# Gated layer over a context of 257 keys: chunks of 128 + 128 + 1 in place of three of 86

## The chip, the cores and the metric

The kernel runs on one core of a Trainium2 chip. The metric is device time in microseconds of the whole program, one launch. Everything is fp32.

## The reference, cut to what matters

```python
def _L0_xattn_ref(x, w1, v1, w2):            # x: (128, 32, 128); all three weights are ctx: (128, 257, 128)
    h1 = jnp.einsum('eth,efh->etf', x, w1)
    h2 = jnp.einsum('eth,efh->etf', x, v1)
    g = jax.nn.gelu(h1, approximate=False) * h2
    return jnp.einsum('etf,efh->eth', g, w2)
...
x = x + _L0_xattn_ref(_layernorm(x, axis=-1), ctx_1024, ctx_1024, ctx_1024)
x = x + _L0_attn_ref(...)      # and four more layers, which the change leaves alone
```

For each of 128 batches, 32 rows of x are normalised and multiplied with the 257 keys of the batch's context, which gives h of 32 by 257. Since h1 and h2 are the same, g is gelu(h) * h. Then g is multiplied with the context again, and the result is added to x.

## The kernel before, in words

The function `stage_ctx_glu` computes this layer. A tile `t` is four batches, 4 x 32 = 128 rows of X, and there are NT = 32 tiles; X stays in SBUF as `k.X` for the whole kernel. The context of a tile is loaded as `cN` ("glu_ctx_N", four buffers in turn), as three chunks of 86 keys (JC = 86, NJ = 3; the 258th is zero) in 96 partitions. The host lays it out in `layouts`.

Per tile, the steps are:

- `ctx_transpose`: TensorE transposes the chunks of each batch (12 a tile, L248) into banks `pC[b]`; ScalarE copies batches 0 and 2 (L308), VectorE 1 and 3 (L359) to `cT`.
- `norm` (VectorE, L353), `transpose` (TensorE, L241) and `copy` (ScalarE, L303) prepare the normalised, transposed rows `xT`.
- `h`: four matmuls (L257) of one batch each, on four groups of 32 columns of the array at once. Each matmul is recorded as two instructions.
- `gelu` (ScalarE, L313) and `gate` (VectorE, L364) make gh.
- `g_transpose`: three transposes (L265), `g_copy` by ScalarE (L318).
- `y`: for each chunk, four matmuls (L274), one a batch, which again run side by side: 12 matmuls, 24 instructions.
- `add`: VectorE adds `y` to X (L109) and takes the statistics of the new X for the next layer (L111).

Each engine runs its own instruction list, and semaphores order them. Within a list the order is written out by hand in `body`. TensorE's is: context transposes of tile t+1, transposes of gh of t, `h` of t+1, `transpose` of t+2, `y` of t. VectorE's is: copies of t+1, `norm` of t+2, `gate` of t+1, `add` of t. The first four tiles and the last four are written out; those between run in a loop of four tiles a round (`tiles`).

X is loaded in four groups of 4, 8, 10 and 10 tiles (GROUPS), all ahead of or between the first four context loads on the one queue of SyncE (SP). `look_at(g)` is VectorE's statistics of a group (L344, L347), and POOL then computes the reciprocal deviation of the group (L403, L405, waited for by `norm` of tiles 0 and 4). `look_at(1)` stands in tile 0 ahead of its `gate`, `look_at(2)` and `look_at(3)` at the start of tiles 1 and 2. A context buffer is loaded again when `y` of its tile is done (L212).

Of the kernel before, what the change touches and what calls it, by code (L numbers as in the profile page):

```python
# [24 lines left out]
P = 128  # L25
# [127 lines left out]

def stage_ctx_glu(nc, k, x, ident, ctxN, ahead):
    JZ = NJ * JC
    with ExitStack() as ctx:
# [5 lines left out]
        def sem(name):  # L162
# [8 lines left out]
        ge = [sb(f"gelu{i}", [P, JZ]) for i in range(2)]  # L171
        gh = [sb(f"gh{i}", [P, JZ]) for i in range(2)]
        gT = [sb(f"gh_T{i}", [JC, NJ * P]) for i in range(2)]
# [4 lines left out]
        x_landed, ident_landed = [sem(f"x_landed{g}") for g in range(len(GROUPS))], sem("ident_landed")  # L178
        stats, means, var_eps, rstd_done, set_up = (sem(n) for n in (
            "stats0", "mean_var_done", "variance_shifted", "rstd_done", "constants_set"))  # L180
# [18 lines left out]
        @block.sync  # L199
        def _(sp):  # L200
            clear_stale(sp, k)

            def load(t, slot):
                sp.dma_start(cN[slot][:, :, :, :], ctxN[t]).then_inc(landed[slot], 16)
# [12 lines left out]

        def tiles(eng, body):

            for t in range(WAYS):  # L220
                body(t, t)
            with eng.Fori(0, NT // WAYS - 2) as i:
                for w in range(WAYS):
                    body(WAYS * i + WAYS + w, w)
            for w in range(WAYS):
                body(NT - WAYS + w, w)
# [10 lines left out]
        def _(pe):  # L237
# [5 lines left out]
            def ctx_transpose(t, slot, b):  # L243
                if b == 0:
                    pe.wait_ge(landed[slot], turn(t, slot))
                wait(pe, (c_even, c_odd)[b % 2], 2 * (t - 1) + b // 2 + 1)
                for c in range(NJ):
                    m = pe.transpose(pC[b][:, c * JC:(c + 1) * JC], cN[slot][0:JC, b, c, :], k.ident[0:JC, 0:JC])  # L248
                m.then_inc(c_turned, 1)

            def h(t, slot):
                pe.wait_ge(xt_ready, t + 1)
                pe.wait_ge(c_even, 2 * t + 2)
                pe.wait_ge(c_odd, 2 * t + 2)
                wait(pe, gh_ready, t)
                for b in range(BT):
                    m = pe.matmul(pH[b * S:(b + 1) * S, 0:JZ], xT[slot % 2][:, b * S:(b + 1) * S],  # L257
                                  cT[slot % 2][:, b, :], start=True, stop=True)
                m.then_inc(h_ready, 1)

            def g_transpose(t, slot):
                pe.wait_ge(gh_ready, t + 1)
                wait(pe, gt_ready, t)
                for c in range(NJ):
                    m = pe.transpose(pG[0:JC, c * P:(c + 1) * P], gh[slot % 2][:, c * JC:(c + 1) * JC], k.ident[:, :])  # L265
                m.then_inc(g_turned, 1)

            def y(t, slot):
                pe.wait_ge(gt_ready, t + 1)
                wait(pe, added, 2 * (t - 1) + 1)  # L270
                for c in range(NJ):
                    for b in range(BT):
                        o = c * P + b * S
                        m = pe.matmul(pY[b * S:(b + 1) * S, 0:D], gT[slot % 2][:, o:o + S],  # L274
                                      cN[slot][0:JC, b, c, :], start=(c == 0), stop=(c == NJ - 1))
                m.then_inc(y_ready, 1)

            def body(t, slot):
                nxt, second = after(t, slot, 1), after(t, slot, 2)
                if isinstance(t, int) and t == 0:  # L280
                    pe.wait_ge(ident_landed, 16)
                    for b in range(BT):
# [12 lines left out]
                y(t, slot)  # L295
# [3 lines left out]
        def _(act):  # L299
# [5 lines left out]
            def ctx_copy(t, slot, b):  # L305
                act.wait_ge(c_turned, BT * t + b + 1)
                wait(act, h_ready, t - 1)
                act.activation(cT[slot % 2][:, b, :], pC[b][:, 0:JZ], ACT.Copy).then_inc(c_even, 1)  # L308

            def gelu(t, slot):  # L310
                act.wait_ge(h_ready, t + 1)
                wait(act, gh_ready, t - 1)
                act.activation(ge[slot % 2][:, :], pH[:, 0:JZ], ACT.Gelu).then_inc(ge_ready, 1)  # L313

            def g_copy(t, slot):
                act.wait_ge(g_turned, t + 1)
                wait(act, y_ready, t - 1)
                act.activation(gT[slot % 2][:, :], pG[0:JC, 0:NJ * P], ACT.Copy).then_inc(gt_ready, 1)  # L318

            def body(t, slot):  # L320
                nxt, second = after(t, slot, 1), after(t, slot, 2)
                if isinstance(t, int) and t == 0:
                    ctx_copy(t, slot, 0)
                    ctx_copy(t, slot, 2)
# [14 lines left out]
        def _(dve):  # L339
# [9 lines left out]
            def norm(t, slot):  # L349
                if isinstance(t, int) and t in (0, 4):  # L350
                    dve.wait_ge(rstd_done, 1 if t == 0 else len(GROUPS))
                wait(dve, turned, t - 1)
# [3 lines left out]
            def ctx_copy(t, slot, b):  # L356
                dve.wait_ge(c_turned, BT * t + b + 1)
                wait(dve, h_ready, t - 1)
                dve.tensor_copy(cT[slot % 2][:, b, :], pC[b][:, 0:JZ]).then_inc(c_odd, 1)  # L359

            def gate(t, slot):
                dve.wait_ge(ge_ready, t + 1)
                wait(dve, g_turned, t - 1)
                dve.tensor_tensor(gh[slot % 2][:, :], ge[slot % 2][:, :], pH[:, 0:JZ], ALU.mult).then_inc(gh_ready, 1)  # L364
# [33 lines left out]
        def _(pool):  # L398
            pool.memset(half_neg[:, :], -0.5).then_inc(set_up, 1)
            pool.wait_ge(set_up, 1)  # L400
            for g, (lo, hi) in enumerate(GROUPS):
# [3 lines left out]
                pool.tensor_tensor(k.RSTD[:, lo:hi], k.SD[:, lo:hi], half_neg[:, lo:hi], ALU.pow).then_inc(rstd_done, 1)  # L405


# [2094 lines left out]
def build(nc, a, out):  # L2502
    with ExitStack() as ctx:
# [21 lines left out]
        with ExitStack() as early:  # L2525
            def eb(name, shape):
# [22 lines left out]
                gqa, ("gqa_wq", "gqa_wkv", "gqa_wout", "gqa_gamma", "gqa_normw", "causal"))]  # L2549
            stage_ctx_glu(nc, k, a["x"], a["ident"], a["ctxN"], for_linear)  # L2550
            deviation_phase(nc, k, "ln2")
# [34 lines left out]
def layouts(i):  # L2586
# [7 lines left out]
    o["ctxT"] = ctx.reshape(NT, BT, JP, D).transpose(0, 3, 1, 2)  # L2594
    ctx_rows = np.zeros((NT, JR, BT, NJ, D), np.float32)
    ctx_rows[:, :JC] = ctx.reshape(NT, BT, NJ, JC, D).transpose(0, 3, 1, 2, 4)
    o["ctxN"] = ctx_rows
    row = np.arange(P)
# [74 lines left out]
```

## Time and profile before

| | |
|---|---|
| median of 3 runs | 2311.27 us (2311.0 to 2311.86) |
| the profiled execution | 2309.65 us, of which its span 2307.9 |
| mean granted TensorE clock over the span | 0.966 |
| busy share of the span | TensorE 92%, VectorE 67%, ScalarE 56%, POOL 45% |
| last VectorE instruction of this stage | starts at 135.40 us |
| first TensorE instruction of the next stage | starts at 138.17 us |

The span is the time from the first instruction of the program to the last. Busy shares are means over all stages. A line such as L257 is a line of the kernel; the same helper line can serve several stages (L109 and L111 do). A matmul's end is modelled, so the starts of TensorE's groups tell more than their ends.

### The profile page before, as it was taken

The page shows a single profiled execution, that of the slowest core. Times are in us where ns is not written, and L with a number is a line of the kernel's source. Part 1 is how long each engine was busy: PE and PEld are TensorE (multiplying, and loading weights), DVE is VectorE, ACT ScalarE, POOL GpSimd, SP SyncE. Part 2 cuts the span into 40 slices and gives each one's busy share as a digit, 9 for nine tenths or more (in the row PEclk, how much of TensorE's full clock was granted, in tenths as well). Part 3 has the DMA queues.
Part 4 walks back from the last instruction along what each step waited for, and adds up shares of the span by engine and source line. Part 5 has one row for each costly group of instructions (what it writes and reads, how often), then busy time and mean ns, then how long its engine had stood idle before and what let it go on. Part 6 is the DMA issues. An engine that isn't in the chain of part 4 may idle for free. (4 is left out here: it accounts for less than half of the span.)

```text
span 2307.9 us, 81023 instructions
## 1 busy us (share of the span) xinstructions
PE 2119.3 (92%) x27948; PEld 1563.2 (68%) x27949; DVE 1535.6 (67%) x5463; ACT 1300.8 (56%) x3747; POOL 1027.1 (45%) x935
## 2 busy tenths in 40 slices
PE   7989999997999899978999999999889999989994
PEld 4657777774677677756777777777556665665992
DVE  4578888874777743347888888888666666754442
ACT  3555555555888433336777777777645555532330
POOL 1024444333888300006555656555266666625115
PEclk9999999997999899988999999999999999979997
DMA  6640000000000000000111111111140000001112
GB/s 161 174 130 1 0 0 0 0 1 1 1 0 0 1 1 0 0 26 25 36 34 34 34 34 34 34 34 34 35 169 0 0 0 0 0 2 41 42 42 77
DMA packets 41208, 71.52 MB, mean 31 GB/s; under 512 B 6176, under 2 KB 30624, under 8 KB 40480
## 3 DMA queue, kind: packets, MB, share of 16 engines
q1 hardware_dynamic: 37792, 63.55, 9.4%
q0 software_dynamic: 3328, 6.82, 0.9%
q8 instruction: 53, 0.87, 0.2%
q14 instruction: 35, 0.29, 0.0%
HBM read 60.91 MB, written 9.44 MB: 30 GB/s over the span
## 5 line engine op out<-in xcount | busy, mean ns | idle before, releaser
L2276 ACT ACTIVATE xat_scores<-xat_scores,xat_least 128x257 f32<-128x257 f32 x512 | 258.5, 505 | 103.5 <-DVE xat_least L2410 102.3
L2410 DVE CUSTOM_DVE_ANT_0 xat_scores<-bank,xat_mask_b 128x257 f32<-128x257 f32 x512 | 207.6, 422 | 88.7 <-PE bank L2120 87.9
L1050 POOL TENSOR_TENSOR gqa_rnorm<-gqa_norm_min,gqa_minus_half 128x12 f32<-128x12 f32 x64 | 145.8, 2278 | 104.9 <-DVE gqa_norm_min L1127 104.9
L2178 PE MATMUL bank<-ident,xat_scores 128*128 128x128 f32 x1024 | 189.2, 287 | 0.0
L2178 PEld LDWEIGHTS bank<-ident,xat_scores 128*128 128x128 f32 x1024 | 116.4, 142 | 81.0 <-issue 49.0
L690 POOL TENSOR_TENSOR lin_q_softmax<-lin_q_exp,lin_q_rsum 128x512 f32<-128x512 f32 x64 | 66.7, 1042 | 223.2 <-DVE lin_q_rsum L751 223.2
L1693 DVE SCALAR_TENSOR_TENSOR X<-bank,expert_shares,X 128x128 f32 (+1 forms) x256 | 72.0, 343 | 130.9 <-PE bank L1607 130.7
L1630 ACT ACTIVATE moe_gelu<-bank 128x512 f32<-128x512 f32 x128 | 76.5, 597 | 146.1 <-PE bank L1597 146.1
L1607 PEld LDWEIGHTS bank<-moe_w,moe_gelu 128*128 128x128 f32 x1024 | 124.2, 192 | 30.8 <-issue 18.2
L1368 POOL TENSOR_TENSOR bat_scores<-bat_scores,bat_max 128x512 f32<-128x512 f32 x128 | 130.5, 1041 | 32.5 <-DVE bat_max L1400 32.5
L1400 DVE CUSTOM_DVE_ANT_0 bat_scores<-bank,bat_causal_add 128x128 f32<-128x128 f32 x512 | 110.7, 286 | 47.2 <-PE bank L1256 47.2
L568 PEld LDWEIGHTS bank<-lin_w_v_out,lin_z_T 128*128 128x128 f32 x1024 | 119.1, 191 | 22.0 <-issue 20.2
L568 PE MATMUL bank<-lin_w_v_out,lin_z_T 128*128 128x128 f32 x1024 | 131.2, 281 | 1.3 <-ACT lin_z_T L620 1.3
L1607 PE MATMUL bank<-moe_w,moe_gelu 128*128 128x128 f32 x1024 | 124.6, 275 | 0.3 <-DVE expert_shares L1680 0.3
L1597 PE MATMUL bank<-ln_T,moe_w 128*128 (+1 forms) x256 | 123.0, 604 | 0.8 <-PEq L1423 0.8
L2295 ACT ACTIVATE xat_p_T<-bank 128x256 f32<-128x256 f32 x256 | 96.4, 377 | 41.3 <-PE bank L2178 38.0
L2342 POOL TENSOR_TENSOR xat_ctx_kept<-xat_keep,xat_ctx_T 128x1028 f32<-128x1028 f32 x32 | 71.0, 2220 | 82.9 <-DMA xat_ctx_T<-in_ctxT 82.8
L2120 PE MATMUL bank<-xat_k_cos,xat_q_blocks 32*128 32x257 f32 x1024 | 92.7, 431 | 16.6 <-DVE xat_least L2410 14.7
L2366 POOL TENSOR_SCALAR xat_keep<-xat_pad 128x1028 f32<-128x1028 uint8 x1 | 1.6, 1552 | 237.6 <-DMA xat_pad<-in_xat_pad 237.6
L2417 DVE COPY xat_p_T<-bank 128x256 f32<-128x256 f32 x256 | 106.7, 417 | 0.2 <-PE bank L2178 0.2
L2276 ACT ACTIVATION_READ_ACCUMULATOR xat_scores<-xat_scores,xat_least 128x1 f32 x512 | 97.6, 191 | 0.0
L2151 PE MATMUL bank<-xat_w_v,xat_ctx_T 128*128 128x128 f32 x512 | 90.2, 299 | 0.0
(320 smaller groups left out, 5826.9 us busy)
## 6 DMA issues: line engine op xcount, KB each, us to landing
glu_ctx_N<-in_ctxN SPq DMA_DIRECT2D x32, 576.0 KB, 4.3
xat_ctx_T<-in_ctxT SPq DMA_DIRECT2D x32, 516.0 KB, 3.6
xat_pad<-in_xat_pad SPq DMA_DIRECT2D x32, 128.5 KB, 3.4
expert_w<-in_glx_w SPq DMA_DIRECT2D x1, 4096.0 KB, 14.9
slot_rows<-gqa_zero_rows SPq DMA_DIRECT2D x1, 2560.0 KB, 11.0
slt_rows<-slot_rows SPq DMA_DIRECT2D x40, 64.0 KB, 1.8
slot_results<-slt_y POOLq DMA_DIRECT2D x40, 64.0 KB, 1.8
moe_w<-in_moe_w SPq DMA_DIRECT2D x2, 1024.0 KB, 5.8
```

The lines of the kernel that those rows point to most:

```text
L568: m = pe.matmul(pY[:, 0:D], zT[slot][:, hd, :], wvo[:, hd // 2, hd % 2, :], start=(hd == 0), stop=(hd == H - 1))
L1050: pool.tensor_tensor(rn[h][:, :], sm[h][:, :], half_neg[:, :], ALU.pow).then_inc(rnorm, 1)
L1368: pool.tensor_tensor(sx[g][:, :, :], sx[g][:, :, :], spread(mx[g][:, :], P), ALU.subtract).then_inc(s_shifted, 1)
L1400: dve.tensor_tensor_reduce(sx[g][:, i, :], pS[g][:, i * P:(i + 1) * P], cadd[:, :], 1.0, -BIG, ALU.add, ALU.max, mx[g][:, i:i + 1]).then_i ...
L1597: pe.matmul(pH[e % 2][c][:, :], w1[:, e, c * P:(c + 1) * P], k.LT[:, ts(b, TB), :], start=True, stop=True).then_inc(h_made, 1)
L1607: m = pe.matmul(pY[e % WAYS][:, i * D:(i + 1) * D], ge[e % 2][:, c, i * P:(i + 1) * P], w2[:, e, c, :], start=(c == 0), stop=(c == NF - 1))
L2120: m = pe.matmul(pS[g][:, 0:J], qb[slot][r, part, j, :, :], keys[j % 2][r, :], start=(part == 0), stop=(part == 1))
L2178: m = pe.transpose(dst[:, c * P:(c + 1) * P], sx[j % 2][:, g, c * P:(c + 1) * P], k.ident[:, :])
L2276: act.activation(sx[j % 2][:, g, :], sx[j % 2][:, g, :], ACT.Exp, bias=mn[j % 2][g][:, 0:1], scale=-1.0, accum_out=sm[j % 2][:, g:g + 1]). ...
L2295: act.activation(pt[j % 2][g][:, :], unit_bank(*at)[:, 0:NC * P], ACT.Copy).then_inc(pa_copied, 1)
L2410: dve.tensor_tensor_reduce(sx[j % 2][:, g, :], pS[g][:, 0:J], mb[slot][:, j, :], 1.0, BIG, ALU.add, ALU.min, mn[j % 2][g][:, 0:1]).then_in ...
L2417: dve.tensor_copy(pt[j % 2][g][:, :], unit_bank(*at)[:, 0:NC * P]).then_inc(pd_copied, 1)
```

## The change

The 257 keys are split as 128 + 128 + 1. The two full chunks take the same way as before, with 8 transposes of the context, 2 of gh and 8 matmuls in `y` a tile. The last key goes another way. Its rows for all 128 batches are loaded once (`lN`, 64 KB), transposed once (`lT`), and POOL puts the four columns of a tile into `cT` (`put_last`), so `h` still has all keys. For `y`, the host lays the last key's row 32 times a batch beside the two chunks (the load stays 576 KB), and VectorE multiplies it with the last column of gh and adds it to X (`add_last`), before `add`. The X groups 2 and 3 are loaded behind all of the first four context tiles, their `look_at` moves to tiles 3 and 4, behind `gate` and `add_last` and ahead of `add`, and `look_at(1)` behind `gate` and `add_last` of tile 0. POOL's deviations follow, and eight tiles are written out at the start instead of four.

```diff
-        cN = [sb(f"ctx_N{i}", [JR, BT, NJ, D]) for i in range(WAYS)]
-        cT = [sb(f"ctx_T{i}", [P, BT, JZ]) for i in range(2)]
+        cN = [sb(f"ctx_N{i}", [P, BT * NC + 1, D]) for i in range(WAYS)]
+        cT = [sb(f"ctx_T{i}", [P, BT, J]) for i in range(2)]
+        lN, lT = sb("last_N", [P, D]), sb("last_T", [P, P])
...
+            sp.dma_start(lN[:, :], ctx_last).then_inc(lasts_landed, 16)
...
-            for t, (lo, hi) in enumerate(GROUPS):
-                sp.dma_start(k.X[:, lo:hi, :], x_rows[:, lo:hi, :]).then_inc(x_landed[t], 16)
-                load(t, t)
+            load_x(0)
+            load(0, 0)
+            load_x(1)
+            load(1, 1)
+            load(2, 2)
+            load(3, 3)
+            load_x(2)
+            load_x(3)
             with sp.Fori(0, NT // WAYS - 1) as i:
                 for w in range(WAYS):
                     sp.wait_ge(y_ready, WAYS * i + w + 1)
+                    sp.wait_ge(last_added, WAYS * i + w + 1)
                     load(WAYS * i + w + WAYS, w)
...
-                for c in range(NJ):
-                    m = pe.transpose(pC[b][:, c * JC:(c + 1) * JC], cN[slot][0:JC, b, c, :], k.ident[0:JC, 0:JC])
+                for c in range(NC):
+                    m = pe.transpose(pC[b][:, c * P:(c + 1) * P], cN[slot][:, b * NC + c, :], k.ident[:, :])
...
+                pe.wait_ge(last_put, t + 1)
                 wait(pe, gh_ready, t)
...
-                for c in range(NJ):
+                for c in range(NC):
                     for b in range(BT):
                         o = c * P + b * S
                         m = pe.matmul(pY[b * S:(b + 1) * S, 0:D], gT[slot % 2][:, o:o + S],
-                                      cN[slot][0:JC, b, c, :], start=(c == 0), stop=(c == NJ - 1))
+                                      cN[slot][:, b * NC + c, :], start=(c == 0), stop=(c == NC - 1))
...
+            def add_last(t, slot):
+                dve.wait_ge(gh_ready, t + 1)
+                dve.scalar_tensor_tensor(out=k.X[:, t, :], in0=cN[slot][:, BT * NC, :], scalar=gh[slot % 2][:, LAST:J],
+                                         in1=k.X[:, t, :], op0=ALU.mult, op1=ALU.add).then_inc(last_added, 1)
 
             def add(t, slot):
                 dve.wait_ge(y_ready, t + 1)
+                dve.wait_ge(last_added, t + 1)
                 residual_tile(dve, k, t, pY[:, 0:D], added, 2 * t)
...
+                    gate(t, slot)
+                    add_last(t, slot)
                     look_at(1)
-                    gate(t, slot)
-                if isinstance(t, int) and 1 <= t < 3:
-                    look_at(t + 1)
...
                 if nxt:
                     gate(*nxt)
+                    add_last(*nxt)
+                if isinstance(t, int) and t in (3, 4):
+                    look_at(t - 1)
...
+            def put_last(t, slot):
+                wait(pool, h_ready, t - 1)
+                pool.tensor_copy(cT[slot % 2][:, :, LAST], lT[:, ts(t, BT)]).then_inc(last_put, 1)
...
+                if isinstance(t, int) and t in (0, 4, 5):
+                    deviation({0: 1, 4: 2, 5: 3}[t])
```

## Rows read from the trace of the kernel before

**Rows 1.** Timeline of one settled tile: start us, us, engine, line, operation
```profile
86.47 0.64 PE L257 MATMUL bank<-glu_ctx_T,glu_xT 128*32 128x258 f32 x8 [0.29 <-issue]
...
87.17 0.39 ACT L313 ACTIVATE glu_gelu<-bank 128x258 f32<-128x258 f32 x1 [0.47 <-PE bank L257]
87.30 0.86 PE L274 MATMUL bank<-glu_ctx_N,glu_gh_T 86*32 86x128 f32 x24
...
87.59 0.42 DVE L364 TENSOR_TENSOR glu_gh<-glu_gelu,bank 128x258 f32<-128x258 f32 x1 [0.97 <-ACT glu_gelu L313]
88.09 1.11 PE L248 MATMUL bank<-ident,glu_ctx_N 86*128 86x86 f32 x12
88.34 0.29 DVE L109 TENSOR_TENSOR X<-X,bank 128x128 f32 x1 [0.33 <-PE bank L274]
...
88.77 0.29 DVE L111 BATCH_NORM_STATS2 bn_stats<-X  x1
...
88.98 0.74 DVE L359 COPY glu_ctx_T<-bank 128x258 f32<-128x258 f32 x2
...
89.82 0.64 PE L257 MATMUL bank<-glu_ctx_T,glu_xT 128*32 128x258 f32 x8 [0.29 <-issue]
```

**Rows 2.** Timeline of ScalarE: the gelu of tile 7 and of tile 31
```profile
49.80 0.39 ACT L313 ACTIVATE glu_gelu<-bank 128x258 f32<-128x258 f32 x1 [0.46 <-PE bank L257]
...
131.32 0.39 ACT L313 ACTIVATE glu_gelu<-bank 128x258 f32<-128x258 f32 x1 [0.57 <-PE bank L257]
```

**Rows 3.** Timeline of an early tile, number 4
```profile
33.13 1.98 PE L248 MATMUL bank<-ident,glu_ctx_N 86*128 86x86 f32 x12
...
35.84 1.09 PE L257 MATMUL bank<-glu_ctx_T,glu_xT 128*32 128x258 f32 x8
...
37.26 1.51 PE L274 MATMUL bank<-glu_ctx_N,glu_gh_T 86*32 86x128 f32 x24
...
37.40 0.42 DVE L364 TENSOR_TENSOR glu_gh<-glu_gelu,bank 128x258 f32<-128x258 f32 x1 [1.56 <-ACT glu_gelu L313]
38.70 1.55 PE L248 MATMUL bank<-ident,glu_ctx_N 86*128 86x86 f32 x9
```

**Rows 4.** Timelines of VectorE and TensorE in the first six tiles
```profile
12.81 0.42 DVE L364 TENSOR_TENSOR glu_gh<-glu_gelu,bank 128x258 f32<-128x258 f32 x1 [0.47 <-ACT glu_gelu L313]
...
14.92 1.09 PE L257 MATMUL bank<-glu_ctx_T,glu_xT 128*32 128x258 f32 x8
...
18.45 2.01 DVE L344 BATCH_NORM_STATS2 bn_stats<-X 128x6 f32<-128x128 f32 x10
...
21.19 0.72 DVE L359 COPY glu_ctx_T<-bank 128x258 f32<-128x258 f32 x2
...
22.17 1.09 PE L257 MATMUL bank<-glu_ctx_T,glu_xT 128*32 128x258 f32 x8 [1.76 <-DVE glu_ctx_T L359]
...
41.26 1.09 PE L257 MATMUL bank<-glu_ctx_T,glu_xT 128*32 128x258 f32 x8
...
45.75 0.64 PE L257 MATMUL bank<-glu_ctx_T,glu_xT 128*32 128x258 f32 x8 [0.30 <-issue]
```

**Rows 5.** Timeline of TensorE in the next stage: transposes of 128 by 128
```profile
158.06 0.60 PE L531 MATMUL bank<-ident,lin_q_softmax 128*128 128x128 f32 x4
```

**Rows 6.** Groups of VectorE by form, cross attention: busy us, mean ns, idle before
```profile
L2430 DVE SCALAR_TENSOR_TENSOR xat_o_mixed<-xat_v,xat_v_last,bank 128x128 f32<-128x128 f32 x128 | 43.4, 339 | 1.2 <-PE bank L2142 1.2
```

**Rows 7.** Timeline of VectorE in the linear attention's loop
```profile
301.32 0.68 DVE L749 TENSOR_REDUCE lin_q_sum<-lin_q_exp 128x8 f32<-128x512 f32 x1
302.03 0.20 DVE L751 RECIPROCAL lin_q_rsum<-lin_q_sum 128x8 f32<-128x8 f32 x1
```

**Rows 8.** Groups of POOL by form
```profile
L1379 POOL TENSOR_SCALAR bat_head_diag_scaled<-bat_head_diag 128x4 f32<-128x4 f32 x1 | 0.2, 198 | 0.1
```

**Rows 9.** The page's DMA issues: count, KB each, median us to landing
```profile
glu_ctx_N<-in_ctxN SPq DMA_DIRECT2D x32, 576.0 KB, 4.3
```

**Rows 10.** A stretch of transposes: us; PE, PEld, DVE, ACT, POOL busy; clock; DMA
```profile
534.00:542.00 8.00, 8.00 (x23) 3.98 (x22) 4.39 (x18) 8.00 (x23) 0.00 (x0) 0.50 0.00 0
```

More of the change, by code:

```diff
@@ L151, in _, with stage_ctx_glu @@
                 dve.tensor_tensor(dst[:, :], k.RSTD[:, :], k.MS[:, :], ALU.mult).then_inc(rc, 1)
-def stage_ctx_glu(nc, k, x, ident, ctxN, ahead):
-    JZ = NJ * JC
+def stage_ctx_glu(nc, k, x, ident, ctxN, ctx_last, ahead):
+    NC, LAST = 2, J - 1
+    JF = NC * P
     with ExitStack() as ctx:
@@ L166, in stage_ctx_glu @@
         WAYS = 4
-        cN = [sb(f"ctx_N{i}", [JR, BT, NJ, D]) for i in range(WAYS)]
-        cT = [sb(f"ctx_T{i}", [P, BT, JZ]) for i in range(2)]
+        cN = [sb(f"ctx_N{i}", [P, BT * NC + 1, D]) for i in range(WAYS)]
+        cT = [sb(f"ctx_T{i}", [P, BT, J]) for i in range(2)]
+        lN, lT = sb("last_N", [P, D]), sb("last_T", [P, P])
         xn = [sb(f"xn{i}", [P, D]) for i in range(2)]
         xT = [sb(f"xT{i}", [P, P]) for i in range(2)]
-        ge = [sb(f"gelu{i}", [P, JZ]) for i in range(2)]
-        gh = [sb(f"gh{i}", [P, JZ]) for i in range(2)]
-        gT = [sb(f"gh_T{i}", [JC, NJ * P]) for i in range(2)]
+        ge = [sb(f"gelu{i}", [P, J]) for i in range(2)]
+        gh = [sb(f"gh{i}", [P, J]) for i in range(2)]
+        gT = [sb(f"gh_T{i}", [P, NC * P]) for i in range(2)]
         pX, pG, pY, pH = k.bank[0], k.bank[5], k.bank[6], k.bank[7]
@@ L218, in tiles @@
         def tiles(eng, body):
-            for t in range(WAYS):
-                body(t, t)
-            with eng.Fori(0, NT // WAYS - 2) as i:
+            for t in range(2 * WAYS):
+                body(t, t % WAYS)
+            with eng.Fori(0, NT // WAYS - 3) as i:
                 for w in range(WAYS):
-                    body(WAYS * i + WAYS + w, w)
+                    body(WAYS * i + 2 * WAYS + w, w)
             for w in range(WAYS):
@@ L254, in h @@
                 pe.wait_ge(c_odd, 2 * t + 2)
+                pe.wait_ge(last_put, t + 1)
                 wait(pe, gh_ready, t)
                 for b in range(BT):
-                    m = pe.matmul(pH[b * S:(b + 1) * S, 0:JZ], xT[slot % 2][:, b * S:(b + 1) * S],
+                    m = pe.matmul(pH[b * S:(b + 1) * S, 0:J], xT[slot % 2][:, b * S:(b + 1) * S],
                                   cT[slot % 2][:, b, :], start=True, stop=True)
@@ L263, in g_transpose @@
                 wait(pe, gt_ready, t)
-                for c in range(NJ):
-                    m = pe.transpose(pG[0:JC, c * P:(c + 1) * P], gh[slot % 2][:, c * JC:(c + 1) * JC], k.ident[:, :])
+                for c in range(NC):
+                    m = pe.transpose(pG[:, c * P:(c + 1) * P], gh[slot % 2][:, c * P:(c + 1) * P], k.ident[:, :])
                 m.then_inc(g_turned, 1)
@@ L270, in y @@
                 wait(pe, added, 2 * (t - 1) + 1)
-                for c in range(NJ):
+                for c in range(NC):
                     for b in range(BT):
@@ L281, in body @@
                     pe.wait_ge(ident_landed, 16)
+                    pe.wait_ge(lasts_landed, 16)
+                    pe.transpose(pG[:, 0:P], lN[:, :], k.ident[:, :]).then_inc(lasts_turned, 1)
                     for b in range(BT):
@@ L307, in ctx_copy @@
                 wait(act, h_ready, t - 1)
-                act.activation(cT[slot % 2][:, b, :], pC[b][:, 0:JZ], ACT.Copy).then_inc(c_even, 1)
+                act.activation(cT[slot % 2][:, b, 0:JF], pC[b][:, 0:JF], ACT.Copy).then_inc(c_even, 1)
             def gelu(t, slot):
@@ L312, in gelu @@
                 wait(act, gh_ready, t - 1)
-                act.activation(ge[slot % 2][:, :], pH[:, 0:JZ], ACT.Gelu).then_inc(ge_ready, 1)
+                act.activation(ge[slot % 2][:, :], pH[:, 0:J], ACT.Gelu).then_inc(ge_ready, 1)
             def g_copy(t, slot):
@@ L317, in g_copy @@
                 wait(act, y_ready, t - 1)
-                act.activation(gT[slot % 2][:, :], pG[0:JC, 0:NJ * P], ACT.Copy).then_inc(gt_ready, 1)
+                act.activation(gT[slot % 2][:, :], pG[:, 0:NC * P], ACT.Copy).then_inc(gt_ready, 1)
             def body(t, slot):
@@ L349, in norm @@
             def norm(t, slot):
-                if isinstance(t, int) and t in (0, 4):
-                    dve.wait_ge(rstd_done, 1 if t == 0 else len(GROUPS))
+                if isinstance(t, int) and t in (0, 4, 8):
+                    dve.wait_ge(rstd_done, {0: 1, 4: 2, 8: len(GROUPS)}[t])
                 wait(dve, turned, t - 1)
@@ L358, in ctx_copy @@
                 wait(dve, h_ready, t - 1)
-                dve.tensor_copy(cT[slot % 2][:, b, :], pC[b][:, 0:JZ]).then_inc(c_odd, 1)
+                dve.tensor_copy(cT[slot % 2][:, b, 0:JF], pC[b][:, 0:JF]).then_inc(c_odd, 1)
             def gate(t, slot):
@@ L400, in _, with deviation @@
             pool.wait_ge(set_up, 1)
-            for g, (lo, hi) in enumerate(GROUPS):
+            def deviation(g):
+                lo, hi = GROUPS[g]
                 pool.wait_ge(means, hi)
@@ L405, in _, with body @@
                 pool.tensor_tensor(k.RSTD[:, lo:hi], k.SD[:, lo:hi], half_neg[:, lo:hi], ALU.pow).then_inc(rstd_done, 1)
+            def put_last(t, slot):
+                wait(pool, h_ready, t - 1)
+                pool.tensor_copy(cT[slot % 2][:, :, LAST], lT[:, ts(t, BT)]).then_inc(last_put, 1)
+            def body(t, slot):
+                nxt = after(t, slot, 1)
+                if isinstance(t, int) and t == 0:
+                    deviation(0)
+                    pool.wait_ge(lasts_copied, 1)
+                    put_last(t, slot)
+                if nxt:
+                    put_last(*nxt)
+                if isinstance(t, int) and t in (0, 4, 5):
+                    deviation({0: 1, 4: 2, 5: 3}[t])
+            tiles(pool, body)
 def unit(t, h):
@@ L2594, in layouts @@
     o["ctxT"] = ctx.reshape(NT, BT, JP, D).transpose(0, 3, 1, 2)
-    ctx_rows = np.zeros((NT, JR, BT, NJ, D), np.float32)
-    ctx_rows[:, :JC] = ctx.reshape(NT, BT, NJ, JC, D).transpose(0, 3, 1, 2, 4)
-    o["ctxN"] = ctx_rows
+    chunks, lasts = g["ctx_1024"][:, :J - 1].reshape(NT, BT, 2, P, D), g["ctx_1024"][:, J - 1]
+    spread_last = np.repeat(lasts.reshape(NT, BT, D), S, axis=1)
+    o["ctxN"] = np.concatenate([chunks.transpose(0, 3, 1, 2, 4).reshape(NT, P, 2 * BT, D), spread_last[:, :, None]], 2)
+    o["ctx_last"] = lasts
     row = np.arange(P)
```

13 lines of the change are left out of this document (10 added, 3 removed).

## The prediction

> **What bounds the kernel now.** The change touches one stage, the first, which holds 32 tiles of the kernel's 81,023 instructions and ends near 135 of 2307.9 us; everything behind it is the same code. So I read that stage alone: first the order of instructions over time for one settled tile, then the same for the first tiles, then single prices elsewhere.
>
> In a settled tile [rows 1] the first TensorE matmul `h` (L257) starts at 86.47 and that of the next tile at 89.82, a period of 3.35 us. Call the start of `h` zero. ScalarE's gelu (L313) starts at 0.70, VectorE's `gate` (L364) at 1.12 and ends at 1.54. TensorE's second matmul `y` (L274) starts at 0.83 and the transposes of the context tile follow at 1.62 (88.09). VectorE's `add` (L109) waits for `y` and starts at 1.87, so VectorE stands idle from 1.54 to 1.87. From there the way is fixed: add, a gap of 0.14, statistics, two copies (L359) from 2.51 to 3.25, and `h` of the next tile 0.10 later. Add to next `h` is 1.48. TensorE's context transposes (1.11 with their tail) and the transposes of gh fit beside that. The reader is to see a ring: h, y, add, statistics, copies, h. TensorE looks nearly full, but only `h`, the transpose between and `y` lie on the ring.
>
> The gelu rows 24 tiles apart [rows 2] give (131.32 - 49.80)/24 = 3.397 us a tile, the same ring with the loop's branch in one tile of four.
>
> The first tiles run at the lower of TensorE's two levels. The granted clock cannot be read there (it is recorded as 1.00 from the start), but the instructions can: 12 context transposes take 1.98 us against 1.11, `y` runs from 37.26 to 38.70, 1.44 against 0.79, and the tile takes 38.70 - 33.13 = 5.57 [rows 1, 3]. There TensorE is the bound. On top come stalls: `look_at` (statistics over a group of X) sits on VectorE ahead of its copies, 18.45 to 21.19, 2.74 us for ten tiles of X, and holds `h` back by 1.76 [rows 4]. The first one in the loop, of eight tiles of X (L377), stands ahead of tile 0's `gate` (12.81), which waits for a gelu that comes late anyway; it costs nothing. `h` starts at 14.92 for tile 1, 22.17 for tile 2, 35.84 for tile 4, 41.26 for tile 5, 45.75 for tile 6 [rows 3, 4] and 0.70 before its gelu, 49.10, for tile 7 [rows 2]. From tile 6 on its eight instructions take 0.64 instead of 1.09: the upper level.
>
> **The change, part by part, settled tiles.**
> Context transposes go from 12 of 86 rows to 8 of 128. Four transposes of 128 by 128 take 0.60 us with their tail [rows 5], so eight take at most 1.20, and less by one tail; against 1.11 that is between -0.1 and +0.1, and it lies off the ring, where TensorE stands still before `h`.
> The transposes of gh go from 3 to 2 and their copy from 384 to 256 columns: off the ring.
> `y` goes from 24 instructions in three rounds of four batches to 16 in two: 0.79 x 1/3 = 0.26 us less, on the ring. `add` could start at 1.87 - 0.26 = 1.61.
> The new `add_last` (VectorE, 128 x 128, with a scalar from each row) stands between `gate` and `add`, and `add` waits for it. The nearest row is the same trick in the cross attention, 339 ns, 128 times [rows 6]. It reads gh, so it waits for `gate`; an instruction that waits for the one before it with one wait starts 0.03 after its end (L749 ends at 302.00, L751 starts at 302.03) [rows 7], with two waits 0.14 after it (88.34 + 0.29 to 88.77) [rows 1]. So `add` starts at 1.54 + 0.03 + 0.34 + 0.03 = 1.94 at best and at 1.54 + 0.14 + 0.34 + 0.14 = 2.16 at worst. That is later than 1.61, and later than today's 1.87: **the ring moves from y to gate, add_last, add.** The period grows by 0.07 to 0.29. `gate` has one wait that matters and in `add` the wait for `add_last` is the last of two, which speaks for the lower end; that the two waits ahead of the statistics do cost 0.14 in every tile of the loop speaks for a bit more. I take 0.13. From tile 7 to tile 31 that is 24 x 0.13 = **+3.1 us** (1.7 to 7.0). The last tile's add stands behind an add_last too, +0.3.
>
> The Trainium skill (VectorE: DVE Perf Modes, section The TRN2 errata) gives an fp32 operation on two tensors (N + 151)/0.96 ns, 291 ns at 128 elements; the trace agrees for L109, 0.29. By that rule add_last would take 0.29 instead of 0.34, and 24 tiles would give 1.2 us less.
>
> POOL's `put_last`, a copy of 4 elements a partition, is bounded by 198 ns from a row of the same size [rows 8] and one tile ahead of its use. In tiles 4 and 5 a `deviation` stands before the next put_last on POOL (about 2.2 us), still 4 us ahead of the `h` that waits for it. If that cover were gone it would cost those 2.2 once. Loads keep their 576 KB and land in 4.3 us [rows 9], while a slot is free three tiles, 10 us, before it is read; the new wait of SP's queue for add_last comes before y is ready, and what is queued behind it is only the next load. The two late X loads have until tile 3. Hidden: nothing.
>
> **The first tiles.** The extra 64 KB (rows of the last key) stands before the first tile's load: about 0.25 us. `gate` of tile 0 ends at 12.81 + 0.42 + 0.27 = 13.5, add_last at 13.9; then the first `look_at`, now behind them, 8/10 of 2.74 = 2.2, then copies and gap 0.85: `h` of tile 1 at 17.0 instead of 14.92, **+2.1**. Tiles at the lower level need 5.57 less 0.48 for `y` less 0.25 for one transpose of gh (1.98/12 for 86 columns, so 0.25 for 128), 4.8. A tile with a `look_at` needs 1.98 to the end of gate (37.40 + 0.42 - 35.84) + 0.37 + 2.74 + 0.32 + 0.21 + 0.84 = 6.5. So tile 5 starts at 17.0 + 3 x 4.8 + 6.5 = 37.9 (before 41.26, **-3.3**), tile 6 at 44.4 (before 45.75), because its look_at now falls where there was none. If TensorE were at its upper level from there, tile 7 would start at 47.9, **-1.2**. But both look_at tiles leave it idle for over 2 us just before, and each tile at the lower level costs 4.8 - 3.5 = 1.3. I count one such tile: +0.1 for the whole start.
>
> Sum: +0.1 + 3.1 + 0.3 = **+3.5 us**. The profiled execution took 2309.65 (2307.9 of span, 1.75 around it), so 2313.2 for the like of it; the median of the three runs is 1.6 higher, 2311.27, hence **2314.8**.
>
> **Rivals.**
> *The long chain on VectorE and a later clock (slower).* Both gaps at 0.14 give 24 x 0.29 = 7.0, +7.4 in all: 2318.7. For it: the loop's waits on register values often show 0.14. Chance 0.2.
> *TensorE stays at its lower level (slower).* The change takes away a third of `y` and leaves the streamed columns of the transposes as they are. A stretch of nothing but transposes ran at clock 0.50 although TensorE was busy for all of its 8.00 us [rows 10]. Each further tile costs 1.3: one more gives +4.8, the bound of 0.2%; all 24, 2314.8 + 30 = 2345. Against it: h and y still come every tile, and once risen the level held through the 24 tiles of [rows 2]. The Trainium skill (TensorE: Matmul & The Clock Gate, Part 4, PE-mode transpose) says that transposes do not count as TensorE work for the clock in the same way; by this rule the rise comes later or not at all, and the trace agrees with its premise by that 0.50. Chance 0.18 for at least one more tile than I count.
> *The opposite: the stalls end sooner and the clock rises early.* With the look_ats moved to tiles 3 and 4, TensorE works without a stall from 17.0 to 34. If it rises there and holds, two or three tiles gain 1.3 each and the start is worth -3 to -5: 2309.5 to 2311.5, no change. Against it are the idle times right behind. Chance 0.12.
> *y's saving shows (faster).* If gate, add_last and their waits took 0.07 instead of 0.40, `add` would follow `y` at 1.61: 24 x -0.26 = -6.2, with -1.2 from the start -7.4: 2303.9. It decides from `add` earlier than 1.82 on. Only an add_last that overlaps its own input would do it. Chance 0.07.
> The forecast itself holds 0.43.
>
> **How the numbers follow.** What a measurement can tell from no change is 0.2%, 4.6 us. Faster: the last rival and a sliver of the early clock, 0.09. Slower by over 4.6: the first two and the upper part of my own range (2311 to 2317), 0.41. Within: 0.50. The range reaches from the early clock, 2309, to the long chain with two or three late tiles, 2322; outside stay y's saving below and a clock that hardly rises above, together under 0.2.
>
> **What would show it.** VectorE: L109's successor starting right behind add_last and no longer waiting for TensorE; period 3.45 to 3.6 where it was 3.40. `y` at 0.53. TensorE's idle time a tile up from 0.3 to 0.7 or more. `h` of tile 1 at 17.0, of tile 5 near 38, of tile 6 near 44. The transposes' 12 to 8 without effect on `h`. Wrong would be: add waiting for `y` as before; a period under 3.35; the level of the clock changing elsewhere than between tiles 5 and 8; POOL or a DMA named before `h`.

## The result and the profile after

The changed kernel takes 2305.59 us (median of 15 runs, 2301.32 to 2310.82), the kernel before 2310.78 on the same chip (15 runs, 2303.7 to 2314.19). The ratio is 0.9982, 95% interval 0.9974 to 0.9991: 0.18% faster, inside the 0.2% that I called no change, but under the lower end of my range, 2309. The profiled execution took 2305.04 us, its span 2303.3.

Timeline of one settled tile after (start us, us, engine, line, operation), the answer to [rows 1]:

```profile
86.55 0.64 PE L273 MATMUL bank<-glu_ctx_T,glu_xT 128*32 128x257 f32 x8 [0.60 <-ACT glu_ctx_T L326]
...
87.25 0.39 ACT L331 ACTIVATE glu_gelu<-bank 128x257 f32<-128x257 f32 x1 [0.87 <-PE bank L273]
87.38 0.38 PEld L290 LDWEIGHTS bank<-glu_ctx_N,glu_gh_T 128*32 128x32 f32 x16
87.38 0.64 PE L290 MATMUL bank<-glu_ctx_N,glu_gh_T 128*32 128x128 f32 x16
87.39 0.19 POOL L439 COPY glu_ctx_T<-glu_last_T 128x4 f32 x1 [3.13 <-PE bank L273]
...
87.67 0.42 DVE L384 TENSOR_TENSOR glu_gh<-glu_gelu,bank 128x257 f32<-128x257 f32 x1 [0.96 <-ACT glu_gelu L331]
...
87.96 1.09 PE L263 MATMUL bank<-ident,glu_ctx_N 128*128 128x128 f32 x8
88.13 0.35 DVE L388 SCALAR_TENSOR_TENSOR X<-glu_ctx_N,glu_gh,X 128x128 f32 x1
...
88.40 0.28 DVE L109 TENSOR_TENSOR X<-X,bank 128x128 f32 x1
...
88.82 0.29 DVE L111 BATCH_NORM_STATS2 bn_stats<-X  x1
...
89.03 0.73 DVE L379 COPY glu_ctx_T<-bank 128x256 f32<-128x256 f32 x2
```

The gate (L384) starts 1.12 after `h`, as before. The `add_last` (L388) follows 0.46 later and takes 0.35, where its row in the cross attention said 0.34 [rows 6]. (The estimate of 0.29 by the formula in the Trainium skill, VectorE: DVE Perf Modes, section The TRN2 errata, is near L109's 0.28, but not near this 0.35.) But `add` (L109) starts 0.27 after the *start* of add_last, 0.08 before its recorded end, at 88.40, which is 1.85 after `h`. Before it stood at 1.87. No releaser stands behind L109 now: it no longer waits for TensorE, only for its turn. The statistics (L111) need the new X and start 0.42 after the start of `add`.

That one VectorE instruction can start before the recorded end of the one ahead could be seen in the kernel before. Timeline of VectorE in its last tiles, which are written out and not in the loop:

```profile
131.74 0.42 DVE L364 TENSOR_TENSOR glu_gh<-glu_gelu,bank 128x258 f32<-128x258 f32 x1 [1.38 <-ACT glu_gelu L313]
132.08 0.28 DVE L109 TENSOR_TENSOR X<-X,bank 128x128 f32<-128x128 f32 x1
132.39 0.29 DVE L111 BATCH_NORM_STATS2 bn_stats<-X 128x6 f32<-128x128 f32 x1
```

The add, which doesn't need this gate's result, starts 0.34 after the start of an instruction of 0.42. And the statistics start 0.03 after the end of add, where the same instructions in the loop show 0.14 [rows 1]. So the number of waits, by which I chose between 0.03 and 0.14, is not what sets that gap.

Timelines of the changed kernel: ScalarE's gelu of tiles 7 and 31, and TensorE's `h` of tiles 1 to 7 (the one number more, [n <-issue], is idle time ahead of it):

```profile
46.22 0.39 ACT L331 ACTIVATE glu_gelu<-bank 128x257 f32<-128x257 f32 x1 [0.73 <-PE bank L273]
...
128.24 0.39 ACT L331 ACTIVATE glu_gelu<-bank 128x257 f32<-128x257 f32 x1 [0.87 <-PE bank L273]
```

```profile
16.08 1.08 PE L273 MATMUL bank<-glu_ctx_T,glu_xT 128*32 128x257 f32 x8 [2.60 <-issue]
...
21.16 0.97 PE L273 MATMUL bank<-glu_ctx_T,glu_xT 128*32 128x257 f32 x8 [0.25 <-issue]
...
24.81 0.64 PE L273 MATMUL bank<-glu_ctx_T,glu_xT 128*32 128x257 f32 x8 [0.60 <-ACT glu_ctx_T L326]
...
28.12 0.64 PE L273 MATMUL bank<-glu_ctx_T,glu_xT 128*32 128x257 f32 x8 [0.60 <-ACT glu_ctx_T L326]
...
34.20 0.64 PE L273 MATMUL bank<-glu_ctx_T,glu_xT 128*32 128x257 f32 x8 [3.35 <-issue]
...
40.24 1.08 PE L273 MATMUL bank<-glu_ctx_T,glu_xT 128*32 128x257 f32 x8 [2.24 <-issue]
...
45.31 0.84 PE L273 MATMUL bank<-glu_ctx_T,glu_xT 128*32 128x257 f32 x8 [0.25 <-issue]
```

The settled period is (128.24 - 46.22)/24 = 3.418 us, against 3.397 [rows 2]: 24 tiles cost +0.5, where I forecast +3.1. This +0.5 doesn't come from `add`: by the gelu rows the two middle tiles of a loop round take 3.32 and 3.31 (before 3.35 and 3.30), but the tile in which the loop turns takes 3.73 and the one behind it 3.42 (before 3.56 and 3.35). In the kernel before with nothing but idle instructions added (the padded kernel below) the turn takes 3.67, so at least a part of this is not the work of the stage. The written-out tiles at both ends give some of it back. Tile 7 starts at 45.31 against 49.10: the start gives -3.8, where I forecast +0.1. In the `h` rows 1.08 is the lower level of the clock (1.2 GHz) and 0.64 the upper (2.4 GHz). TensorE reached the upper one at 21.9 us, worked in it (`h` of tile 2 to 3 took 3.65 us, 3 to 4 took 3.31), fell back at 35.5 during the two look_at tiles (34.20 - 28.12 = 6.08, then 6.04) and rose again at 45.8. The granted clock of two windows of the changed kernel says the same (columns: stretch; its length; busy PE, PEld, DVE, ACT, POOL; clock; DMA share and GB/s):

```profile
30.00:45.00 15.00, 9.40 (x78) 6.29 (x76) 11.10 (x59) 4.30 (x12) 4.80 (x7) 0.68 0.33 102
45.00:60.00 15.00, 12.21 (x158) 7.71 (x161) 9.25 (x30) 7.55 (x23) 0.96 (x5) 0.97 0.54 168
```

The stage's last VectorE instruction starts at 132.71 (135.40 before), -2.7. Nothing behind it was changed, and there the executions scatter by themselves. The mark for the end of the stage is the start of ScalarE's L129 (`std`): 137.15 before, 134.46 after. From it to the end of the span it is 2170.8 us before, 2168.8 after, and 2167.4 to 2173.4 in four profiles below (those without the long last stage told of there, the padded kernel left out). So each experiment is read at the end of the stage first. One part of it is not scatter. From this mark to the next `std` (L133, 528.8 before) the changed kernel, the chunks alone and the kernel with the extra matmuls need 393.1 to 393.6 us in four profiles, all others 391.0 to 392.0; the changed kernel's clock is at 0.50 from 156 to 158 us, the one before at 1.00. What brings that fall is not shown.

### The profile page after: what moved, and what is told of

Read it like the earlier page. It is cut to its first block and busy times, and to the rows that moved or that the text cites. A ratio compares the mean times of both kernels' runs of the same rounds, so it can differ in the third digit from the quotient of the medians.

```text
span 2303.3 us, 80324 instructions
## 1 busy us (share of the span) xinstructions
PE 2102.4 (91%) x27533; PEld 1549.2 (67%) x27534; DVE 1543.0 (67%) x5495; ACT 1297.1 (56%) x3748; POOL 1032.8 (45%) x967
## 5 line engine op out<-in xcount | busy, mean ns | idle before, releaser
L2166 PE MATMUL bank<-xat_k_cos,xat_q_blocks 32*128 32x257 f32 x1024 | 92.7, 431 | 16.6 <-DVE xat_least L2456 14.7
```

The costliest lines, as they stand in the source:

```text
L2166: m = pe.matmul(pS[g][:, 0:J], qb[slot][r, part, j, :, :], keys[j % 2][r, :], start=(part == 0), stop=(part == 1))
```

## The experiments

Twelve runs follow. They were taken in four sittings, and in two of them every profile shows a last stage of 295 to 301 us where it is 258 to 260 otherwise; the median of the kernel before was 2349.5 to 2349.9 there. (Runs under one chip number show both; why it is so stays open.) Ratios are to the kernel before in the same sitting.

**Once more the changed kernel.**

> The kernel after, unchanged, to have it beside the others on one chip. Stage one ends (first instruction of the deviation behind it) at 134.5 us as before, give or take one early tile at the other clock level (2.2 us); ratio to before 0.998.

2343.69, ratio 0.9972 (0.9963 to 0.9981), stage end 133.62. Clock: up at 20.9, down at 34.5, up at 44.8, as in the first profile. Only here there was one more short rise ahead of it: `h` of tile 1 already took 0.64, at 16.26, and the level was lost at 17.5. So the pattern repeats in the main, with 0.8 us between two stage ends of the same kernel.

**add_last ahead of the next gate.**

```diff
                 if second:
                     norm(*second)
+                add_last(t, slot)
                 if nxt:
                     gate(*nxt)
-                    add_last(*nxt)
```

> The kernel after with one move: add_last of tile t stands ahead of gate of tile t+1, in VectorE's idle time, instead of gate and add_last of t+1 ahead of add of t. Theory A (add of tile t does not wait for the add_last in front of it, whose tile is the next one; it only stands behind it in VectorE's queue, at 0.27 us, and y is done before): add then follows y at about 1.6 us after h instead of 1.85, the settled period falls from 3.43 to about 3.1 us, 24 tiles give -8 us against the kernel after, near 2298. Theory B (h is held by ScalarE's copies, as the wait's name says, and VectorE's queue does not matter): period stays at 3.4, no difference.

2339.89, ratio 0.9963 (0.9948 to 0.9977), stage end 126.28. Timeline of a settled tile, and the gelu of tiles 7 and 31:

```profile
78.68 0.64 PE L273 MATMUL bank<-glu_ctx_T,glu_xT 128*32 128x257 f32 x8 [0.35 <-ACT glu_ctx_T L326]
78.75 0.35 DVE L388 SCALAR_TENSOR_TENSOR X<-glu_ctx_N,glu_gh,X 128x128 f32 x1
...
79.51 0.64 PE L290 MATMUL bank<-glu_ctx_N,glu_gh_T 128*32 128x128 f32 x16
...
79.80 0.42 DVE L384 TENSOR_TENSOR glu_gh<-glu_gelu,bank 128x257 f32<-128x257 f32 x1 [0.70 <-ACT glu_gelu L331]
...
80.22 0.29 DVE L109 TENSOR_TENSOR X<-X,bank 128x128 f32 x1
```

```profile
44.77 0.39 ACT L331 ACTIVATE glu_gelu<-bank 128x257 f32<-128x257 f32 x1 [0.73 <-PE bank L273]
...
120.32 0.39 ACT L331 ACTIVATE glu_gelu<-bank 128x257 f32<-128x257 f32 x1 [0.77 <-PE bank L273]
```

The period falls to 3.148. `add` stands 1.54 after `h`, right behind the gate, and add_last runs in VectorE's idle time while `h` is under way. So what the changed kernel pays is the place of add_last in the queue, 0.27 us a tile, and that eats up what the change had gained there, 3.397 - 3.148 = 0.25.

**Without add_last** (the last key's share of `y` is left out, and with it the two waits for add_last).

```diff
                 if nxt:
                     gate(*nxt)
-                    add_last(*nxt)
```

> The kernel after without add_last: the last key's share of y is left out, h and gelu still have it. Theory A: the same as with add_last moved, period about 3.1, -8 us against the kernel after; the difference of the two is what the moved add_last still costs, at most 0.05 us a tile. Theory B: period stays at 3.4.

2419.71, ratio 1.0302 (1.0274 to 1.0331): 70 us slower than the kernel before, although the stage ended at 125.62 with a period of 3.175. All the loss lay in the cross attention, 712 us instead of 636, whose code I had not touched. (The cross attention is taken from the first transpose of its rows to the `std` behind it, 1031.3 to 1667.1 in the kernel before.) That was unexplained then.

**The order alone**: the loads, the look_ats and the eight written-out tiles of the change, with the old chunks of 86.

```diff
-            for t, (lo, hi) in enumerate(GROUPS):
-                sp.dma_start(k.X[:, lo:hi, :], x_rows[:, lo:hi, :]).then_inc(x_landed[t], 16)
-                load(t, t)
+            load_x(0)
+            load(0, 0)
+            load_x(1)
+            load(1, 1)
+            load(2, 2)
+            load(3, 3)
+            load_x(2)
+            load_x(3)
```

> The kernel before (three chunks of 86) with only the order of the change: late X loads behind the four context loads, look_at of groups 2 and 3 in tiles 3 and 4 behind gate, look_at of group 1 behind the first gate, eight tiles written out. Theory C (the order alone brings the early gain, because TensorE works without a stall in tiles 1 to 4 and rises to its upper level): settled period 3.40 as before, tile 7 starts 2 us or more earlier than 49.1. Theory D (it is the work taken off TensorE and the faster loads in 128 partitions): with tiles of 5.57 and two of 7.2, and 17.0 for tile 1, tile 7 starts near 51 and the kernel is 1 to 3 us slower than before.

2433.87, ratio 1.0361 (1.0344 to 1.0379). The same loss in the cross attention (715 us), and the first stage ended 5.0 us *later* than before, at 142.13.

**The chunks alone**: the new chunks, last key included, with the old order of loads and look_ats.

> The kernel after with the loads, look_at and deviations in the order of the kernel before: the chunks alone. Theory C: the stalls of tiles 1 and 2 come back (h of tiles 2 and 3 about 7 us apart each), tile 7 starts at 48 to 50, settled period 3.43, so the kernel is level with before or up to 1 us slower. Theory D: tile 7 starts near 46, and the kernel is as fast as the kernel after. Context loads in 128 partitions land faster than in 96 in both.

2343.9, ratio 0.9977 (0.9968 to 0.9987). Timelines of ScalarE, and of TensorE's `h` of tiles 1 to 4:

```profile
42.61 0.39 ACT L331 ACTIVATE glu_gelu<-bank 128x257 f32<-128x257 f32 x1 [0.89 <-PE bank L273]
...
124.64 0.39 ACT L331 ACTIVATE glu_gelu<-bank 128x257 f32<-128x257 f32 x1 [0.88 <-PE bank L273]
...
130.87 0.32 ACT L129 ACTIVATE std<-mean_var,eps 128x32 f32<-128x32 f32 x1
```

```profile
13.54 0.96 PE L273 MATMUL bank<-glu_ctx_T,glu_xT 128*32 128x257 f32 x8 [0.39 <-issue]
...
19.90 0.64 PE L273 MATMUL bank<-glu_ctx_T,glu_xT 128*32 128x257 f32 x8 [3.32 <-issue]
...
25.94 1.09 PE L273 MATMUL bank<-glu_ctx_T,glu_xT 128*32 128x257 f32 x8 [2.07 <-issue]
...
31.92 0.64 PE L273 MATMUL bank<-glu_ctx_T,glu_xT 128*32 128x257 f32 x8 [0.36 <-issue]
```

Its stage ended 6.3 us ahead of the kernel before (5.7 by a second profile of that one), and 2.8 to 3.6 ahead of the full change. So the gain is the chunks'; the new order takes about half of it back. Most of that stands already at `h` of tile 1, 13.54 against 16.08 in the changed kernel: the first look_at, moved behind the gate. The upper level comes early in the old order too: it was there from about 14 to 21 us, was lost at the look_ats, and came back for good at 31. The whole times don't separate this run from the changed kernel; the stage does.

**Eight more matmuls on TensorE while it waits for the first context tile.**

```diff
+                    for _ in range(8):
+                        pe.matmul(pY[:, 0:P], k.ident[:, :], lN[:, :], start=True, stop=True)
```

> The kernel after with eight extra matmuls of 128 columns (each two instructions, 0.2 us each at the lower level, 3.4 us in all) on data that has landed, in the time before the first context tile lands at 7.0. If only TensorE's level makes the first tiles slow and it rises with such work: the first context transposes already take 1.1 us instead of 2.0 and stage one ends 2 to 4 us earlier than 134.5. If the stalls of VectorE set the first tiles: under 1 us.

2342.26, ratio 0.9969 (0.9959 to 0.998), stage end 134.14. The upper level was there at 7.8 us, and was lost again at 14.6. Timeline of TensorE:

```profile
9.84 0.64 PE L273 MATMUL bank<-glu_ctx_T,glu_xT 128*32 128x257 f32 x8
...
15.71 1.09 PE L273 MATMUL bank<-glu_ctx_T,glu_xT 128*32 128x257 f32 x8 [2.97 <-issue]
```

`h` of tile 0 ran at the upper level, that of tile 1 at the lower one, behind 2.97 us of idle time under `look_at(1)`. Here the early rise was worth nothing: the stage ended between the two ends of the unchanged kernel (133.62 and 134.46), since VectorE stopped TensorE right behind it.

**The statistics in pieces.** On top of the earlier add_last: look_at(1) ahead of tile 0's gate again, and groups 2 and 3 four X tiles at a time in tiles 1 to 5. (The waits for POOL's deviations follow; they and the move of look_at(1) are not among the lines shown.)

```diff
+                add_last(t, slot)
+                if isinstance(t, int) and 1 <= t < 6:
+                    look_at(2 if t < 3 else 3, (8 + 4 * t, 12 + 4 * t))
                 if nxt:
                     gate(*nxt)
-                    add_last(*nxt)
-                if isinstance(t, int) and t in (3, 4):
-                    look_at(t - 1)
```

> add_last moved ahead of the next gate as in the run before, and the statistics of groups 2 and 3 of X taken four tiles at a time in VectorE's idle time of tiles 1 to 5, group 1 again ahead of the first gate. Theory A (what costs in the first tiles is the place of look_at on VectorE): no stall of 2.7 us in tiles 4 and 5 and none in tile 0, tile 7 starts near 38 instead of 44.1, stage one ends near 120 instead of 126.3, 14 us ahead of the kernel after. Rival (TensorE's level decides the first tiles and is lost and won by chance): within 3 us of 126.3.

2324.22 against 2349.55, ratio 0.9887 (0.9872 to 0.9903), stage end 115.93. Once more, on another chip, where the last stage is not the long one:

> The fastest version once more, unchanged, on another chip. If its 0.9887 is its own and not the chip's, the first stage ends at 115 to 117 us again, the later stages take what they take in the kernel before, and the ratio is 0.987 to 0.991. If the rest of the gain (about 26 us in all, of which the first stage explains 21) came from the chip's long last stage, the ratio is 0.9905 to 0.9915 here.

2287.87 against 2310.71, ratio 0.9897 (0.988 to 0.9913). Timelines of VectorE ahead of tile 2's gate, and of ScalarE at the stage's end:

```profile
18.32 0.35 DVE L388 SCALAR_TENSOR_TENSOR X<-glu_ctx_N,glu_gh,X 128x128 f32<-128x128 f32 x1
18.59 0.87 DVE L364 BATCH_NORM_STATS2 bn_stats<-X 128x6 f32<-128x128 f32 x4
19.48 0.38 DVE L367 BATCH_NORM_AGGREGATE mean_var<-bn_stats 128x2 f32<-128x6 f32 x4
19.78 0.39 DVE L384 TENSOR_TENSOR glu_gh<-glu_gelu,bank 128x257 f32<-128x257 f32 x1
...
116.65 0.32 ACT L129 ACTIVATE std<-mean_var,eps 128x32 f32<-128x32 f32 x1
```

A piece nearly fits between add_last and the gate, which would wait for its gelu there anyway: the gelu ends at 19.45, and the gate starts 0.33 later. TensorE's `h` then waits for 0.56 us at most in these tiles, the clock rises at 16.4 and stays up to the last tile, and the tiles are 3.2 to 3.3 us apart from tile 2 to tile 8. The stage is 20 us shorter than before, of which the period gives 24 x 0.25 = 6. With the earlier add_last alone it ended at 126.28, so look_at(1)'s old place and the pieces together give about 10; they were not tried apart. This version is 1% faster than the kernel before and 0.8% than the changed one.

**Where a loop lies in its engine's code.** The two kernels with the slow cross attention had one thing in common: VectorE's instruction list (the program text, not the executed count) is 2396 long. The one before has 2359, the changed one 2428. To move the code and nothing else:

```diff
             dve.memset(k.eps[:, 0:1], EPS)
+            for i in range(37):
+                dve.memset(scratch[:, i:i + 1], 0.0)
```

> The kernel before with 37 memsets of single scratch columns on VectorE at the very start, where it waits for X anyway. VectorE's list then has 2396 instructions, the same number as in the two kernels (no add_last; order only) whose cross attention took 713 and 716 us instead of 636; no buffer, wait or work of any later stage differs from the kernel before. Theory P (the place of VectorE's loop in its instruction list decides whether the loop's instructions are fetched again in each round): the cross attention goes to 710 to 720 us, the page's q14 instruction packets from 35 to about 100, and the whole to 2420 to 2432 us, ratio 1.030 to 1.036. Theory Q (what the two kernels changed in stage one, buffers or semaphores or clock, does it): 2349 to 2353, ratio 1.000 to 1.0015.

2391.07 against 2309.5, ratio 1.0347 (1.0327 to 1.0368), cross attention 715 us against 636. The kernel before, with 37 idle memsets at its start, loses 80 us 1000 us later. Of the DMA queues on the pages of the profile, before and padded:

```profile
q14 instruction: 35, 0.29, 0.0%
```

```profile
q14 instruction: 100, 0.82, 0.1%
```

Groups of VectorE from 1100 to 1600 us, the same instruction in both kernels (L2410 is L2413 in the padded one): busy us, mean ns, idle before it and by what:

```profile
L2410 DVE CUSTOM_DVE_ANT_0 xat_scores<-bank,xat_mask_b 128x257 f32<-128x257 f32 x417 | 169.4, 422 | 69.5 <-PE bank L2120 68.8 <-issue 0.3
```

```profile
L2413 DVE CUSTOM_DVE_ANT_0 xat_scores<-bank,xat_mask_b 128x257 f32<-128x257 f32 x361 | 146.6, 422 | 120.5 <-PE bank L2123 65.6 <-issue 54.9
```

54.9 us of "issue" where there were 0.3: time in which the engine waited for nothing that another had to do. They come as two stops in each round of the loop, 3.06 us ahead of 1277.80 and 1.67 ahead of 1279.90 for one. A round takes 44.4 instead of 38.3 us, and the granted clock of a round falls to 0.92, as windows of one round each show, before and padded:

```profile
1190.00:1228.30 38.30, 37.51 (x416) 27.54 (x414) 31.01 (x130) 29.59 (x108) 22.86 (x14) 1.00 0.12 34
```

```profile
1190.00:1234.40 44.40, 40.05 (x414) 29.09 (x414) 30.79 (x128) 29.67 (x107) 22.70 (x14) 0.92 0.11 31
```

The other way round, 32 memsets for the order alone and for the kernel without add_last, so that both have 2428 again:

> The order of loads and look_ats of the changed kernel on the old chunks of 86, as in the order-only kernel, with 32 memsets of scratch columns on VectorE at the start, so that its list has 2428 instructions like the changed kernel's. Theory P: cross attention back at 636 us, the stage one that was 5.0 us longer stays 4 to 6 longer, so the whole is 3 to 6 above the kernel before: ratio 1.0013 to 1.0026. Theory Q: as the order-only kernel, ratio 1.036.

> The changed kernel without add_last (the last key's share of y is left out of the result), with 32 memsets of scratch columns on VectorE at the start to put every later instruction back to its place in the changed kernel. Theory P: cross attention 636 us; stage one ends near 125.6 as in the run without add_last, 9 us ahead of the changed kernel, so about 2334 to 2338, ratio 0.993 to 0.9955. Theory Q: 2420, ratio 1.030. This run also gives what add_last costs where it stands: the difference to the changed kernel's 2343.7.

The order alone: 2311.85, ratio 1.0009 (0.9999 to 1.0018), stage end 145.12. Without add_last: 2297.74, ratio 0.9943 (0.9926 to 0.9961), stage end 126.64. Both cross attentions are back at 636 us, with 36 and 37 instruction packets, so the place was all of it. That the engine has to load the loop's instructions again in each round is my reading of the packets; no run shows it by itself. Timeline of TensorE in the order alone:

```profile
39.33 1.09 PE L266 MATMUL bank<-glu_ctx_T,glu_xT 128*32 128x258 f32 x8 [0.67 <-DVE glu_ctx_T L368]
...
62.04 1.09 PE L266 MATMUL bank<-glu_ctx_T,glu_xT 128*32 128x258 f32 x8
...
64.83 1.11 PE L257 MATMUL bank<-ident,glu_ctx_N 86*128 86x86 f32 x12
```

With the old chunks and the new order the stalls are nearly gone (1.25 ahead of `h` of tile 1, then 0.67 at most), yet the upper level comes only at 64.7 (57.8 without the memsets), where it came at 42.5 to 43.8 in the kernel before; until then each tile takes 5.6 us, 6.2 with a look_at. That is the price of the order, +5.0 and +8.0 in two runs.

The kernel before, once more:

> The kernel before, for its profile on the same chip as the others. Both theories: cross attention about 636 us, first stage to about 137, 35 q14 instruction packets.

2309.1, stage end 136.57, clock up at 42.5, 35 instruction packets.

## Why the prediction was wrong, by its own steps

**The step that failed: "the ring moves from y to gate, add_last, add".** I let `add` wait for the add_last in front of it. The code says otherwise: `add` of tile t waits for `last_added` of t + 1, which is the add_last of its *own* tile, done one tile earlier. The add_last in front of it belongs to the next tile and touches another tile of X. So there were no two waits and no full 0.34 between them, only 0.27 from start to start (88.13 to 88.40). Instead of 1.94 to 2.16, `add` comes at 1.85, and the forecast 0.13 a tile becomes 0.02, which is what remains of the loop's longer turns: +0.5 in place of +3.1. The ring did move, as forecast: L109 has no releaser, `y` is shorter (0.58 from its start to the next group's, for 0.79; forecast 0.53), and without add_last in that place the period is 3.15 to 3.19. So the direction of each part was right, and the 0.26 for `y` near; the dependence was misread, one tile off. That 1.85 then lies so near the old 1.87 is chance: two sums of other terms that happen to meet.

**The first tiles, +0.1: mis-sized, -3.8.** The tile times at the lower level were near: 5.08 and 5.07 where I had 4.8. The look_at tiles took 6.08 and 6.04 where I had 6.5 for both at the lower level; the first of them ran at the upper one up to 35.5. What I left to a rival was the clock, which rose at 21.9, ahead of any late look_at: from tile 2 to 3 and from 3 to 4 it took 3.65 and 3.31 instead of 4.8, -2.6 together. The rest against my numbers is -0.9 for `h` of tile 1 (16.08 for 17.0), -0.9 for the look_at tiles and +0.5 for the other two. The -0.9 of tile 1 is there at the gelu of tile 0 already, which came at 11.77 where it had been 12.39 and I had added 0.25.

**The rivals.** "The stalls end sooner and the clock rises early" fits the start in its number, -3 to -5, but by luck: the level was lost again at the look_ats, and the moved look_ats are not the cause. (A level that changes elsewhere than between tiles 5 and 8 was one of my signs of being wrong, and it came.) With the old order the new chunks gain more, 6.3 us at the stage's end, and have the upper level from 14 us on for a while; with the old chunks the new order loses 5 to 8. Shown is that each part has this sign. What sets the clock's first rise stays open. With the old chunks and the new order it comes later than before, although TensorE stands still less; and an early rise is not the new chunks' alone, for the padded kernel before had one too, from 16.6 to 23.4 us. "y's saving shows" failed in the changed kernel, and its mechanism, an add_last that doesn't stand between, is what the earlier add_last makes true. The long chain did not occur, and the level was upper from 45.8 to the end of the stage's tiles, no later than I had counted.

**Costed at nothing, and nothing seen:** POOL's put_last (0.19 us, a tile ahead), the loads, the transposes of the context (1.09 for 1.11). The last tile: `h` of tile 31 is 3.1 earlier and the stage's end 2.7, so +0.4, where I had +0.3.

**Sum:** -3.8 + 0.5 + 0.4 = -2.9 against the -2.7 of the stage; the 0.2 is that the gelu of tile 7, from which the period is counted, came only 3.6 earlier. The median fell by 5.2. The other 2.5 us lie in stages that the change leaves alone, in spite of the 1.7 more in the next one, and are within what executions of one code differ by there, so I claim no cause for them. Of the 9.2 us between 2314.8 and 2305.59, then, 6.2 are the stage (+3.5 forecast, -2.7 measured), 2.5 are the rest of the program, and 0.5 is that the kernel before itself came at 2310.78 and not 2311.27. Even without those last two the stage alone would have led to 2308.6, below my range.

## What to carry to other kernels

Before an operation is priced as a link of a chain, read which instance its semaphore count names; one in front in the same queue that nobody waits for cost its distance to the next start here (0.27), and moved into the engine's idle time it cost nothing that could be seen (3.148 with it, 3.175 and 3.188 without). Long bookkeeping on a copying engine was best cut into pieces that nearly fit its waits: in every profile here in which the upper level came ahead of a look_at in one piece, it was lost at or behind one. And when a stage that nobody touched gets slower, look at "issue" waits and instruction packets before looking for a cause in the data.

## What was not expected of the hardware

- The place of a loop in an engine's code: 37 more instructions 1000 us ahead made VectorE stop for about 3.1 and 1.7 us in each round, 100 instruction packets in place of 35, +80 us. With 2359 instructions in the list, and with 2427 or 2428, it doesn't happen; with 2396 it does (three kernels, 100 or 101 packets); other lengths were not tried.
- An independent VectorE instruction starts before the recorded end of the one ahead: 0.27 after the start of one of 0.35.
- The 576 KB of a tile land sooner in 128 rather than 96 partitions. The order of the loads is not the cause: it is 3.8 with the new chunks in the old order, 4.4 with the old chunks in the new order. From the DMA issues on the profile's page, 4.3 us in [rows 9] and after:

```profile
glu_ctx_N<-in_ctxN SPq DMA_DIRECT2D x32, 576.0 KB, 3.8
```
